# Between the gated loop and the FP4 layer: permutation matrix, first weight rows and low-rank product at other places

## The reference

```
z2 = z.reshape(1024, 512)
xq = nvfp4_qdq(z2[:, up_reorder_index], 128)       # scale from max|x| of the whole tensor, blocks of 16
wg = nvfp4_qdq(w_gate[:, up_reorder_index], 128)   # 1376 x 512
wu = nvfp4_qdq(w_up[:, up_reorder_index], 128)
h  = silu(xq @ wg.T) * (xq @ wu.T)
hq = nvfp4_qdq(h[:, down_reorder_index], 128)
out = x + hq @ nvfp4_qdq(w_down[:, down_reorder_index], 128).T * mlp_output_scale + z2 @ lr_A @ lr_B
```

## Time and profile before

| | |
|---|---|
| median of three runs | 858.9 us |
| the profiled execution | 862.48 us, its span 861.2 us |
| PE busy | 736.4 us (86%) |
| DVE busy | 579.2 us (67%) |
| ACT busy | 430.6 us (50%) |
| POOL busy | 189.9 us (22%) |

### The profile page before, as it was taken

One profiled execution on the slowest core, in us unless ns is written; L12 is line 12 of the kernel. 1 busy time (PEld: TensorE's weight loads), 2 busy tenths in 40 slices (PEclk: granted clock), 3 DMA queues, 4 the chain that ended last, 5 costly groups with the idle time before them and its releaser, 6 DMA issues.

```text
span 861.2 us, 11244 instructions
## 1 busy us (share of the span) xinstructions
PE 736.4 (86%) x4112; PEld 545.7 (63%) x4112; DVE 579.2 (67%) x1107; ACT 430.6 (50%) x549; POOL 189.9 (22%) x176
## 2 busy tenths in 40 slices
PE   1797754988999988999999898586799799959998
PEld 1564421656777666766766677474578688957886
DVE  4899977563686867889788586754644333567873
ACT  3756665555876847797877111252243121224452
POOL 0223000021253433355354463032011000000000
PEclk9999855889999999999999999887599899997999
DMA  7644668775375647576663110111111010200001
GB/s 275 208 138 169 214 197 285 242 233 181 125 231 183 199 169 241 174 249 214 225 198 118 58 38 21 51 49 54 45 33 41 21 46 25 67 17 12 25 25 37
DMA packets 56039, 110.55 MB, mean 128 GB/s; under 512 B 9888, under 2 KB 20800, under 8 KB 55984
## 3 DMA queue, kind: packets, MB, share of 16 engines
q1 hardware_dynamic: 42560, 78.43, 28.1%
q10 hardware_dynamic: 9040, 17.30, 6.0%
q0 software_dynamic: 4384, 14.09, 5.6%
HBM read 91.65 MB, written 18.15 MB: 128 GB/s over the span
## 4 chain that ended last, share of the span: by engine, by line
PE 57%; DVE 23%; DMA 7%; ACT 6%; issue 6%; SPq 1%; ACTq 0%; DVEq 0%
PE bank L1110 15%; PE bank L1111 14%; PE bank L1112 14%; PE bank L1213 3%; DVE hot L1747 2%; ACT hot L1501 2%; PE bank L1394 2%; DVE bank L1773 2%; PE bank L1226 1%; DMA wide_buf<-in_down_flat 1%; DMA codes<-c 1%; DVE gm L1789 1%; DVE x L1870 1%; DVE x L1711 1%; PE bank L1243 1%
## 5 line engine op out<-in xcount | busy, mean ns | idle before, releaser
L1501 ACT ACTIVATE hot<-rep,levels 128x2048 f16<-128x2048 f16 x96 | 193.6, 2057 | 19.6 <-ACT c L1464 10.3
L1110 PE MATMUL bank<-zt_h,w_h 128*128 128x512 f32 (+1 forms) x232 | 96.4, 415 | 4.5 <-DVE x L1870 2.5
L1111 PE MATMUL bank<-zt_l,w_h 128*128 128x512 f32 (+1 forms) x232 | 93.3, 402 | 0.0
L1112 PE MATMUL bank<-zt_h,w_l 128*128 128x512 f32 (+1 forms) x232 | 93.2, 402 | 0.0
L1213 PE MATMUL bank<-hot,diag 128*32 128x512 f16 x1160 | 82.3, 412 | 7.7 <-DVE hot L1747 4.9
L1110 PE MATMUL bank<-w_h,xq_h 128*128 128x512 f32 (+1 forms) x192 | 74.7, 389 | 4.6 <-DVE w_l L1888 4.6
L1111 PE MATMUL bank<-w_l,xq_h 128*128 128x512 f32 (+1 forms) x192 | 72.6, 378 | 0.0
L1112 PE MATMUL bank<-w_h,xq_l 128*128 128x512 f32 (+1 forms) x192 | 72.6, 378 | 0.0
L2013 POOL TENSOR_TENSOR q_a<-q_a,q_m 128x384 f32<-128x384 f32 (+3 forms) x34 | 37.0, 1089 | 112.8 <-DVE q_m L1641 112.7
L1985 DVE TENSOR_TENSOR hid<-hid,bank 128x512 f32<-128x512 f32 (+1 forms) x24 | 15.1, 628 | 67.3 <-PE bank L1112 43.6
L1213 PEld LDWEIGHTS bank<-hot,diag 128*32 128x32 f16 x1160 | 26.7, 100 | 53.1 <-issue 26.7
(11 more groups left out here) (219 smaller groups left out, 1676.1 us busy)
## 6 DMA issues: line engine op xcount, KB each, us to landing
rep<-codes SPq DMA_DIRECT2D x58, 512.0 KB, 4.8
codes<-c SPq DMA_DIRECT2D x29, 256.0 KB, 4.6
raw<-in_codes_gu_t ACTq DMA_DIRECT2D x14, 512.0 KB, 5.6
sc<-in_scales_gu_t SPq DMA_DIRECT2D x56, 128.0 KB, 3.9
raw<-in_codes_attn_t ACTq DMA_DIRECT2D x8, 512.0 KB, 4.4
raw<-in_codes_down_t ACTq DMA_DIRECT2D x7, 512.0 KB, 5.7
sc<-in_scales_down_t SPq DMA_DIRECT2D x28, 128.0 KB, 3.2
wide_buf<-in_gate_flat SPq DMA_DIRECT2D x5, 512.0 KB, 4.2
```

What stands on the lines that cost most here:

```text
L1110: PE.matmul(psum, lh, rh, start=first, stop=False, **kw)
L1111: PE.matmul(psum, lh, rl, start=False, stop=False, **kw)
L1112: return PE.matmul(psum, ll, rh, start=False, stop=last, **kw)
L1501: S.activation(hots[plan.slot[hot_ring(t), (t, m)]][:], codes_in_place(t), ACT.Relu, bias=bias, scale=slope).then_inc(sem("ramp_act"), 1)
```

## The change

- In `("d", 6, 1)` no norms stand between the tiles any more; the first two steps of `norm4` come behind the loop, and `known(3, 1)` only where the fifth norm asks for it.
- `perm` (tables, permutation matrix) and the first gathers of `fetch_pair(0)` stand ahead of `("d", 6, 0)`, behind all of the FP4 weights' work. SP and POOL wait there for the last NF4 weights (`weights_end`). The permutation matrix lies in the second half of `xq_l` instead of `wring[2][0]`. `FP4_RATE` goes from 0.72 to 0.8.
- `fetch_pair(0)` has three buffers instead of two and runs beside the permuted products, one row tile for each token tile; a split stands one step behind its transposes, in all three `fetch_pair`s. The copies of the low-rank weights are a step of their own, `lr`, behind the fourth token tile.
- `low_a(0)` stands ahead of the maximum's PE work and `low_a(1)` behind it; their results are taken in steps 1 and 2 of `turned_tiles`, and two `low_b` stand behind the `hmm` of each of the steps 3 to 6. `fetch_pair(1)` starts in step 7.
- `fetch_pair(2)` runs at 1.25 steps for each `hmm` instead of 2.

```diff
-FP4_RATE = 0.72
-FETCH_RATE = 1.5
-FETCH_LATER = 6
+FP4_RATE = 0.8
...
+    first_fetch = fetch_pair(0)
+    for what, g, half in order:
+        until(last_of["gu" if what == "gu" else "down", g])
+        if (what, g, half) == ("d", NG - 1, 0):
+            drain(fp4)
+            p.add("perm")
+            p.sends("perm_in", "perm", 2)
+            p.sends("lr_in", "lr", 2)
+            next(first_fetch)
+        for _ in (gate_up if what == "gu" else down)(g, half):
+            side_nf4.step()
+            side_fp4.step()
+        through.add((what, g, half))
+    for _ in range(normed):
+        next(norm4)
...
     def fetch_pair(c):
-        ring, size = ("row", 2) if c == 0 else ("late", 4)
+        ring, size = ("row", 3) if c == 0 else ("late", 4)
...
             if i + size < len(rows[c]):
                 gather_row(i + size)
+            if i:
+                p.add("rowsplit", c, i - 1)
             yield
-            p.add("rowsplit", c, i)
-            yield
+        p.add("rowsplit", c, len(rows[c]) - 1)
+        yield
...
-    weave(permuted(), Side(itertools.chain(range(FETCH_LATER), first_fetch), FETCH_RATE))
+    for step, _ in enumerate(permuted()):
+        if step == HN:
+            p.add("lr")
+        if step:
+            next(first_fetch, None)
+    drain(first_fetch)
     p.add("xmax")
...
-    low = low_rank()
+    low_a(0)
     greatest_of_all("x")
+    low_a(1)
     p.add("scale", "x", 0, NT)
...
-    first_hidden, second, left, low_left = hidden(0), None, NT, NT + 2
+    first_hidden, low, second = hidden(0), low_rank(), fetch_pair(1)
+    low_left = NT + 2
     for step, _ in enumerate(turned_tiles([("x", n, 0) for n in range(NT)])):
...
         if step >= 3:
             next(first_hidden)
-            left -= 1
-        if second is None:
-            for _ in range(4):
-                if low_left:
-                    next(low)
-                    low_left -= 1
-            if not low_left and step >= 2:
+        for _ in range(2 if step >= 3 else step > 0):
+            if low_left:
+                next(low)
+                low_left -= 1
+            else:
                 drain(low)
-                second = fetch_pair(1)
...
+                next(second, None)
...
-    weave(hidden(1), Side(third, 2))
+    weave(hidden(1), Side(third, 1.25))
...
+    def weights_end(queue):
+
+        queue.wait_ge(*done("pe", "spent", 2 * len(jobs) - 1, LOOK_ORDER[-1]))
+        queue.wait_ge(*done("pe", "made", 2 * len(jobs) - 1))
+        queue.wait_ge(*done("dve", "made", 2 * len(jobs) - 1))
...
             elif kind == "perm":
+                weights_end(sp)
                 SP.dma_start(channel[:], a["c_channel"]).then_inc(dma_sem("perm"), 16)
```

More of the change, by code:

```diff
@@ L631, in down @@
                 stats(3, n)
-                if n % HN == HN - 1:
-                    known(3, half)
-    norm4, normed = norm_turn(3), 0
+                if n == HN - 1:
+                    known(3, 0)
+    norm4, normed = norm_turn(3), 2
     side_nf4, side_fp4 = Side(ready_nf4, NF4_RATE), Side(fp4, FP4_RATE)
@@ L640, in make_plan @@
         order += [("d", g, 0)] + [("gu", g + 1, 0)] * nxt + [("d", g, 1)] + [("gu", g + 1, 1)] * nxt
[L641 to L670, removed]
+    rows = [[(name, t) for name in ("up", "gate") for t in range(f0 // P, (f0 + w + P - 1) // P)] for f0, w in CHUNKS]
     p.rows = rows
     def fetch_pair(c):
-        ring, size = ("row", 2) if c == 0 else ("late", 4)
+        ring, size = ("row", 3) if c == 0 else ("late", 4)
         def gather_row(i):
@@ L688, in fetch_pair, with turn4, main4 @@
                 gather_row(i + size)
+            if i:
+                p.add("rowsplit", c, i - 1)
             yield
-            p.add("rowsplit", c, i)
-            yield
+        p.add("rowsplit", c, len(rows[c]) - 1)
+        yield
+    def turn4(key, *freed_by):
+        p.take("turn4", 4, key, *freed_by)
+    def main4(key, *freed_by):
+        p.take("main4", 4, key, *freed_by)
+    first_fetch = fetch_pair(0)
[13 more added lines that the diff above has]
+        next(norm4)
+    p.turn4 = p.turns % 2
+    p.inherit("turn4", [("turn", 2, p.turn4), ("code", 2, 0), ("code", 2, 1), ("turn", 2, 1 - p.turn4)])
+    p.inherit("main4", [("main", 3, 0), ("main", 3, 1), ("main", 3, 2), ("lora", 1, 0)])
+    p.add("phase")
+    p.turn_in4 = set()
+    p.add("minus")
     def norm4_rest():
@@ L727, in turn_bank, with low_a @@
         turn4(key, *freed_by)
-    first_fetch = fetch_pair(0)
-    next(first_fetch)
-    weave(permuted(), Side(itertools.chain(range(FETCH_LATER), first_fetch), FETCH_RATE))
+    for step, _ in enumerate(permuted()):
[4 more added lines that the diff above has]
+    drain(first_fetch)
     p.add("xmax")
+    def low_a(half):
+        p.add("low_a", half)
+        main4(("la", half), ("dve", "low_take", half))
     def low_rank():
         for half in range(2):
-            p.add("low_a", half)
-            main4(("la", half), ("dve", "low_a", half))
+            p.add("low_take", half)
             yield
@@ L986, in build @@
     zp = hid[:].rearrange("p n f -> p (n f)")[:, NT * (FF - D):].rearrange("p (n d) -> p n d", n=NT)
-    spare = [hid[:, n, D:2 * D] for n in range(5)]
-    pf, pi = spare[0], spare[1].bitcast(I32)
+    pf, pi = hid[:, 0, D:2 * D], hid[:, 1, D:2 * D].bitcast(I32)
+    perm = [xq_l[:, k, HT:T] for k in range(KD)]
     lrw = hid[:, 2, D:D + KD * LR + D]
     zt_flat = [z[:].rearrange("p k t -> p (k t)") for z in (zt_h, zt_l)]
-    row_bufs = spare[3:5]
+    row_bufs = hid[:, 3, 0:D], hid[:, 3, D:2 * D], hid[:, 4, 0:D]
     late_bufs = [z.bitcast(F32)[:, 4 * D + D * i:4 * D + D * (i + 1)] for z in zt_flat for i in range(2)]
     hq = [tuple(z[:, i * D:(i + 1) * D].rearrange("p (f c) -> p f c", c=P) for z in zt_flat) for i in range(4)]
-    perm, lrs = wring[2][0], w_more
+    lrs = w_more
     lt = [[v[0:LR, 2 + half, :] for v in lrs] for half in range(2)]
@@ L1117, in phase_ends @@
         queue.wait_ge(*done("pe", "wturn", "down", len(CHUNKS) - 1, KD - 1))
-        queue.wait_ge(*done("pe", "spent", 2 * len(jobs) - 1, LOOK_ORDER[-1]))
-        queue.wait_ge(*done("pe", "made", 2 * len(jobs) - 1))
+        weights_end(queue)
         queue.wait_ge(*done("act", "cast", len(jobs) - 1))
-        queue.wait_ge(*done("dve", "made", 2 * len(jobs) - 1))
         for name in ("gate", "up", "down"):
@@ L1351, in pe_program @@
                 for k in range(KD):
-                    PE.matmul(bank[:], zt_h[:, k, tok(n)], perm[:, k, :], start=k == 0, stop=False)
-                    last = PE.matmul(bank[:], zt_l[:, k, tok(n)], perm[:, k, :], start=False, stop=k == KD - 1)
+                    PE.matmul(bank[:], zt_h[:, k, tok(n)], perm[k], start=k == 0, stop=False)
+                    last = PE.matmul(bank[:], zt_l[:, k, tok(n)], perm[k], start=False, stop=k == KD - 1)
                 last.then_inc(sem("pprod_pe"), 1)
@@ L1379, in pe_program @@
                 bank, (lh, ll), tc = main4(("lb", n)), lt[n // HN], tok(n % HN)
-                pe.wait_ge(*done("dve", "low_a", 1))
+                pe.wait_ge(*done("dve", "low_take", 1))
                 for m in vacant("main4", ("lb", n)):
@@ L1536, in act_program @@
                 phase_ends(act)
-            elif kind == "perm":
+            elif kind == "lr":
                 act.wait_ge(*landed("lr"))
                 S.copy(lrs[0][:, 0, 0:KD * LR], lrw[:, 0:KD * LR])
-                S.copy(lrs[0][0:LR, 1, :], lrw[0:LR, KD * LR:]).then_inc(sem("perm_act"), 1)
+                S.copy(lrs[0][0:LR, 1, :], lrw[0:LR, KD * LR:]).then_inc(sem("lr_act"), 1)
             elif kind == "rowsplit":
@@ L1554, in act_program @@
                 S.copy(zp[:, n, :], main4(("p", n))[:]).then_inc(sem("ptake_act"), 1)
-            elif kind == "low_a":
+            elif kind == "low_take":
                 half, = key
                 act.wait_ge(*done("pe", "low_a", half))
-                S.copy(lt[half][0], main4(("la", half))[0:LR, :]).then_inc(sem("low_a_act"), 1)
+                S.copy(lt[half][0], main4(("la", half))[0:LR, :]).then_inc(sem("low_take_act"), 1)
             elif kind == "round":
@@ L1595, in act_program @@
                     act.wait_ge(*done("act", "kept", "x", under - 1, 0))
+                act.wait_ge(*done("pe", "rowturn", 0, len(plan.rows[0]) - 1))
                 if c:
-                    act.wait_ge(*done("pe", "rowturn", 0, len(plan.rows[0]) - 1))
-                    act.wait_ge(*done("pool", "perm"))
+                    act.wait_ge(*done("pool", "lr"))
                     act.wait_ge(*done("dve", "perm"))
@@ L1877, in dve_program @@
                 for k in range(KD):
-                    last = V.tensor_scalar(perm[:, k, :], pf, channel[:, k:k + 1], None, ALU.is_equal)
+                    last = V.tensor_scalar(perm[k], pf, channel[:, k:k + 1], None, ALU.is_equal)
                 last.then_inc(sem("perm_dve"), 1)
@@ L1899, in dve_program @@
```

(15 more changed lines are left out.)

10 lines of the change are left out of this document (1 added, 9 removed).

## The result

| | kernel before | changed kernel |
|---|---|---|
| first measurement, median | 859.25 us | 870.89 us (869.45 to 874.28, 4 runs) |
| ratio | | 1.0126 (1.0085 to 1.0167) |
| second measurement, median | 860.73 us (21 runs) | 871.65 us (6 runs) |
| ratio | | 1.0117 (1.0077 to 1.0156) |
| profiled execution | 862.48 us, span 861.2 | 869.45 us, span 868.1 |

Slower, as forecast, but by 11.6 and 10.9 us between the medians (10.8 by the ratio of the first measurement) where I had said 3.7, and outside the range. The profiled executions lie 7.0 us apart; they carry the comparison of the traces.

What follows compares the result with a forecast made beforehand. PE bounds the product stretch; ahead of it lies a chain through DVE, ACT and PE. -7.8 + 1.7 - 19.4 + 27.1 + 2.1 = +3.7 us: 866.2 for the profiled execution, median 862.6, range 850.5 to 868.

Steps and rivals of the forecast that it cites:

- 1, the early matrix: Tables and permutation matrix ahead of the last down products: first `pprod` 7.8 us earlier, at 554.3.
- 2 and 3: Row transposes beside the norms: 1.7 us later at the last `pprod`; maximum's chain to the first `round` unchanged, 6.1.
- 4: From the first `round` to the first `hmm`: 13.5 us instead of 32.9, so 19.4 earlier.
- 5(a) and (b), the waits: Eight `hmm` stages: eight `low_b` add 5.8 us; waits for DVE and banks, with the table load, 15.7.
- 5(c), the clock: Eight `hmm` stages: clock falls at all four stalls, 1.7 us lost each, 6.8 in all, bounds 0 and 10.
- 5(a) and (d): Eight `hmm` stages: eight `low_b` add 5.8 us; two fewer row transposes and a vanished 0.55 wait give -1.2.
- 6, the tail: Behind the eighth `hmm`: 2.1 us longer, since a split now stands a step behind its transposes.
- 7, the FP4 rate: `FP4_RATE` change, FP4 work packed 11% tighter on a busy DVE: 0 us, bounds -2 and +5.
- rival B: Same places and waits in the `hmm` stages, but the clock holds: -3.1 us, median 855.8; chance 0.24.
- C: Rival: `hmm` needn't wait for banks, so neither waits nor clock falls: -18.8 us, 840.1; chance 0.05.
- D: Rival: denser FP4 work gives PE new waits in 300 to 500: +5 on the forecast, 867.6; chance 0.13.
- E: Rival: clock falls at only about half the stalls, or chains 0.8 shorter: about 859.2, no change; chance 0.13.

Runs made afterwards that it cites:

- the repeated run: The changed kernel measured again with no edit: 871.65 us, ratio 1.0117 to the kernel before.
- the version without waits: Changed kernel with `low_add` two `low_b` later and `low_b` taking banks from the other ring (`turn4`): 846.14 us, ratio 0.9834 to the kernel before.

## Why the prediction was right or wrong

- **1, the early matrix.** Right in mechanism: DVE stood 4.40 us for the tables and then was one chain to the first `tsplit`. The timeline of DVE in the changed kernel answers to the earlier trace rows:

```profile
531.51 0.69 DVE L1787 TENSOR_TENSOR w_l<-bank,w_h 128x512 fp32r<-128x512 f32 x1 [1.17 <-ACT w_h L1511]
536.60 0.43 DVE L1877 CAST hid<-hid 128x512 f32<-128x512 int32 x1 [4.40 <-DMA hid<-in_up_idx]
```

  554.88 against 554.3. Partly by luck: two errors cancelled in it. Everything up to the two `tsplit` came 1.4 earlier (the last down products start at 532.30 against 533.66), and from there to the first `pprod` lie 3.0 us (551.89 to 554.88) instead of the 1.0 of my sum. PE does four transposes in them and then stands idle for 1.08 us, for which the trace names no releaser. That the transposes are cold (1.09 long) isn't the reason: in the repeated run they are warm (0.63) and the `pprod` starts 2.3 us behind their start, here 2.2. The 0.3 for shared DMA engines wasn't there: DVE waited 4.40, the sum's own figure.
- **2 and 3.** 22.1 us from the first `pprod` to the end of the last, as worked out (20.3 before plus 1.7); 5.8 from there to the first `round`, against 6.1 before.
- **4.** First `hmm` at 596.27, forecast "near 596", and 13.5 us behind the first `round`, as summed. Right.
- **5(a) and (b), the waits.** Both predicted, at both places, for the reasons given, four times each. I had 15.7 us, they are 13.6: the pieces are 1.78 and 1.27 (2.68 with the table load), not 2.1 and 1.5.
- **5(c), the clock: the step that failed.** The falls came where I put them, four of four; their price was too low. I took 1.7 us for each, from the one fall at 477.55, where 3.4 us ran at 1.2 GHz: 6.8 in all, with 10 as the upper bound. It is 12.1 against the version without waits. By the granted clocks of the four rows above, 5.5, 4.8, 4.4 and 4.1 us of the four `hmm` ran at 1.2 GHz; against the same four without waits they lose 2.5, 2.2, 2.0 and 1.8, 8.5 together. The other 3.5 I hadn't counted: the `qturn` between the two waits is cold as well (1.9), and 1.6 lie around the waits. `take` and silu stand behind that `qturn`, so what it loses moves the start of the `hmm` too.
- **5(a) and (d).** Together 5.7 instead of 4.6, since a `low_b` takes 0.79 and not 0.73, and the first `hmm` is 0.4 longer than before. The sum 5.7 + 13.6 + 12.1 = 31.4 for the eight stages, where I had 27.1.
- **6, the tail.** 681.26 to 688.66 is 7.4 against 5.2: +2.2, forecast 2.1.
- **7, the FP4 rate.** "I take 0" was right for the rate alone, shown. That it was needed for step 1, I had not seen.
- **The remainder.** Up to the ninth `hmm` the traces differ by 8.5, forecast 3.7. The 4.8 between are the clock term (+5.3), the waits (-2.1), 5(a) and (d) (+1.1), the first `hmm` (+0.4) and the tail (+0.1). Behind it 1.6 come back, 181.0 against 179.4 to the end, where I had 0: the ninth and tenth `hmm` with what stands between them take 12.8 us at a granted clock of 0.87, before 14.3 at 0.81. That gives the 7.0 us of the profiled executions. It is no gain of the change that any run shows.
- **From 7.0 to the medians.** The kernel before had been profiled in an execution 3.6 above its median, and the changed one in its fastest. "I carry the difference over" is where the second half of the miss lies: timed executions of the kernel before spread from 856.8 to 868.1 over 21 runs. With the traces' whole difference of 7.0 in place of my 3.7 I would have written 865.9, which still lies within the range up to 868; measured were 870.89. Why the one program's executions differ so much was not tested.
- **The two rules of the Trainium skill ("TensorE: Matmul & The Clock Gate").** By the section "A second HAM failure mode: psum-queue depth-cycling" short idles between groups of matmuls make the clock swing, and this trace agrees: four falls with idles of 1.27 to 2.68 us, granted clock 0.80. The section "HAM oscillation — how this bites in real kernels" with its long gaps would alone have given rival B, 855.8, which the trace doesn't bear out. Neither says which short idle brings the clock down, and these runs don't either. The clearest case is one that I had read as a rule: ahead of the last down products PE waits 2.76 us in eleven of the traces. In the kernel before the clock stayed at 1.00 over the 7 us behind it; in the changed kernel the first matmul there is cold:

```profile
532.30 0.76 PE L1108 MATMUL bank<-w_h,at_h 128*128 128x512 f32 x1 [2.76 <-issue]
```

  In eight of the eleven the granted clock of those 7 us is below 1.00 (0.56 to 0.76), in three it is 1.00. So "after 2.76 at 533.66 it stayed up" was one execution's outcome, and weak evidence for rival B.

The rivals: B needed a held clock (0.80 measured). C needed no wait. D's place, 300 to 500, shows no net loss: the loop ended sooner. E is outside the interval.

## What to carry to other kernels

When work is put into gaps of a doubly buffered stream, look at two orders at once: how many places of the buffer ring it takes between two users of the stream, and behind which instruction its consumer stands in an in-order queue. Either was worth 16.7 us here and both 25.5, while the places that the change was made for had gained 25. Price a clock fall from several executions: here the same wait brought one in some and none in others. A wait in front of an in-order engine should be for something that has long landed: the same tables, loaded at the same time and used 11 us later in DVE's list, gave 3.7 us more (3.5 between the traces).

## What had not been expected of the hardware

- The clock can fall well behind the idle time. After one PE idle of 2.73 us the next matmul was warm (0.47 us), and 1.5 us later the matmuls were 0.63 long; that `hmm` had a granted clock of 0.77. The length of the first matmul alone doesn't tell.
- One and the same wait of 2.76 us, ahead of the same products, was followed by a low clock in eight of eleven traces. Waits of 1.77 or 1.78 and of 1.27 us (2.68 the first time) with four transposes between them had one four times of four; with either kind alone, it fell once of four. Taking away either kind gave back 9.3 or 9.4 us beyond the wait itself.
- In the products behind such a pair 12, 11, 10 and 9 of the 24 matmuls are cold (a granted clock of 0.67 to 0.73 over each product): 8.3 to 7.5 us instead of 5.6 to 5.8.
